# Scores, maxima and weighing of an attention stage in one tile shape of 64 rows by 32 columns, with two banks for the sums

## What is computed

```python
def _L0_xattn_ref(q, k, v, Wq, bq, Wk, bk, Wv, bv, Wo, bo):
    HEADS, D_K = 16, 16
    qh = (q @ Wq + bq).reshape(B, LQ, HEADS, D_K).transpose(0, 2, 1, 3)
    kh = (k @ Wk + bk).reshape(B, LKV, HEADS, D_K).transpose(0, 2, 1, 3)
    vh = (v @ Wv + bv).reshape(B, LKV, HEADS, D_K).transpose(0, 2, 1, 3)
    scores = jnp.einsum('bhqd,bhkd->bhqk', qh, kh) * scale
    attn = jax.nn.softmax(scores, axis=-1)
    ...
x = x + _L0_xattn_ref(_layernorm(x, axis=-1), ctx_512, ctx_512, ...)   # LQ = 256, LKV = 4096
```

## Time and profile before

| | us |
|---|---|
| median of three runs | 1431.7 |
| lowest and highest | 1428.06 and 1433.41 |
| profiled execution, its time | 1427.45 |
| profiled execution, its span | 1425.7 |
| PE busy | 1372.8 (96%) |
| DVE busy | 1070.9 (75%) |
| ACT busy | 962.1 (67%) |
| POOL busy | 287.7 (20%) |

### The profile page before, as it was taken

How to read it: one execution, slowest core, us unless ns; L and a number is a source line. 1 busy time by engine, 2 the same in 40 slices (tenths; PEclk the granted TensorE clock), 3 DMA queues, 4 the chain that set the end, 5 groups by cost and what they waited for, 6 DMA issues and landing times.

```text
span 1425.7 us, 32607 instructions
## 1 busy us (share of the span) xinstructions
PE 1372.8 (96%) x13186; PEld 757.5 (53%) x13186; DVE 1070.9 (75%) x2114; ACT 962.1 (67%) x1931; POOL 287.7 (20%) x321
## 2 busy tenths in 40 slices
PE   7799999999999999999999999998989999989998
PEld 4344444444444444444444545456547999856666
DVE  4787877778787778777778888835876768767757
ACT  5377777777777777777777666672896664448731
POOL 3353121222212222121222100000003100001210
PEclk9899999999999999999999999999999999999999
DMA  5865453335445335544424632002401320347000
GB/s 172 191 160 151 119 134 93 90 92 135 115 122 121 73 90 128 131 113 106 112 68 102 192 83 46 2 1 60 119 24 59 111 68 0 92 117 151 2 1 30
DMA packets 98790, 134.53 MB, mean 94 GB/s; under 512 B 11024, under 2 KB 74128, under 8 KB 92688
## 3 DMA queue, kind: packets, MB, share of 16 engines
q1 hardware_dynamic: 98640, 132.45, 36.8%
HBM read 94.15 MB, written 38.27 MB: 93 GB/s over the span
## 4 chain that ended last, share of the span: by engine, by line
PE 83%; DVE 7%; ACT 7%; issue 2%; DMA 1%; POOL 0%; SPq 0%; DVEq 0%; ACTq 0%; POOLq 0%
PE psum L546 19%; PE psum L566 18%; PE psum L527 7%; PE psum L592 4%; PE psum L632 4%; PE psum L2147 4%; PE psum L2121 3%; PE psum L1241 2%; PE psum L2866 2%; DVE peaks L693 1%; ACT probs L791 1%; ACT key_f L824 1%; PE psum L2876 1%; PE psum L275 1%; PE psum L1638 1%
## 5 line engine op out<-in xcount | busy, mean ns | idle before, releaser
L693 DVE TENSOR_REDUCE peaks<-psum 128x1 f32<-128x512 f32 x1024 | 654.6, 685 | 168.7 <-PE psum L527 157.1
L791 ACT ACTIVATE probs<-psum 128x512 f32<-128x512 f32 x1024 | 555.9, 595 | 126.8 <-PE psum L546 125.0
L546 PE MATMUL psum<-queriesT,keysT 64*128 64x256 bf16 (+1 forms) x4096 | 331.9, 272 | 11.0 <-ACT probs L791 9.8
L566 PE MATMUL psum<-probs,values 128*17 128x256 f32 x4096 | 320.5, 385 | 0.0
L546 PEld LDWEIGHTS psum<-queriesT,keysT 64*128 64x128 bf16 (+1 forms) x4096 | 171.9, 94 | 219.4 <-ACT probs L791 159.3
L527 PE MATMUL psum<-keysT,queriesT 64*128 64x512 bf16 x1024 | 210.2, 379 | 7.3 <-DVE peaks L693 4.0
L566 PEld LDWEIGHTS psum<-probs,values 128*17 128x17 f32 x4096 | 68.0, 95 | 160.4 <-issue 151.3
L927 POOL CAST key_parts<-key_f 128x512 bf16<-128x512 f32 x57 | 34.9, 612 | 516.0 <-ACT key_f L824 509.7
L592 PE MATMUL psum<-ctxT,wk 128*128 128x512 f32 x128 | 75.1, 670 | 2.2 <-DVE probs L736 0.9
L527 PEld LDWEIGHTS psum<-keysT,queriesT 64*128 64x128 bf16 x1024 | 59.8, 94 | 26.1 <-DVE peaks L693 17.5
L632 PE MATMUL psum<-wv,ctxT 128*128 128x256 f32 x256 | 72.0, 407 | 0.5 <-DVE probs L724 0.4
(11 more groups left out here) (315 smaller groups left out, 1647.7 us busy)
## 6 DMA issues: line engine op xcount, KB each, us to landing
keysT<-key_parts SPq DMA_DIRECT2D x186, 256.0 KB, 5.5
key_parts<-key_parts SPq DMA_DIRECT2D x90, 256.0 KB
ctx_nat<-in_ctx_dram SPq DMA_DIRECT2D x32, 256.0 KB, 3.2
ctx_in<-in_ctx_dram SPq DMA_DIRECT2D x24, 256.0 KB, 3.1
ctx_turned<-ctxT SPq DMA_DIRECT2D x24, 256.0 KB, 6.0
ctx_T<-ctx_turned SPq DMA_DIRECT2D x12, 512.0 KB, 3.9
qk_parts<-early_weights SPq DMA_DIRECT2D x24, 128.0 KB
q_parts<-q_parts SPq DMA_DIRECT2D x20, 128.0 KB
```

What stands on the lines that cost most here:

```text
L546: made = e.matmul(ps[j][:, e2 * S:(e2 + 1) * S], self.keysT[own, plane, i % RING, kt * P:(kt + 1) * P], self.queriesT[own, plane, u % 2, g ...
L566: made = e.matmul(k.bank(SUMS)[32 * quad:32 * quad + DH + 1, 0:S], self.values[b % 2][:, kt, g * GH + j, :], self.probs[:, (SLOTS * i + p) ...
L693: e.tensor_reduce(self.peaks[:, i % 2, j * QT + qt, c:c + 1], k.ps(("max", n)), AX.X, ALU.max).then_inc(*self.peaked.up(n))
L791: e.activation(self.probs[:, t % RINGP, 2 * j * S:(2 * j + 2) * S], k.ps(("scores", t, j)), ACT.Exp).then_inc(*self.exped.up((t, j)))
```

## The change

Scores, maxima and weighing all become matmuls of tiles with 64 rows and 32 columns. A score matmul of 128 keys is written as four of 32 (`STRIP`), a maximum of 128 queries as four of 32. Weighing of one slot is split over its 128 keys: first one half of the rows, then, behind a wait for it (`half_weighed`), the other, both adding to the same sums.

The order within a slot is new. One head is early and one late, in turn from slot to slot (`order`). PE writes the early head's first score step, the half of weighing on the other head's rows, the early head's three other steps, the maxima, two steps of the late head, the other half of weighing, and the last two steps. ACT takes the exponentials in the same order.

The sums have two banks, 3 and 4, in turn by group; copying them no longer holds up the next group's weighing. Three banks (5 to 7) are left for maxima and other jobs. DVE clears the second bank at slot 0. Both maxima of a pair now wait for their banks before either is written.

```diff
-SCORES, SUMS, BLOCK = (0, 1, 2), 3, 1
+HALVES, SUMS, STRIP = 3, (3, 4), P // 4
...
+def order(t):
+
+    return (0, 1) if t % 2 else (1, 0)
...
-            choice = (7, 0, 1, 2) if t < -1 else (4, 5, 6, 7)
+            choice = (7, 0, 1, 2) if t < -1 else (5, 6, 7)
...
-        def find_max(n, now):
-            i, j, qt, c = self.max_at(n)
+        def find_maxima(n, now):
+            ps = {}
+            for j in range(GH):
+                job, let_go = ("max", n + j), (self.peaked, n + j)
+                ps[j] = banks.use(4 + (n + j) % 3, w, job, let_go) if now < -1 else misc(now, job, let_go)
...
-            e.matmul(ps, self.queriesT[own, MAIN, u % 2, g, qt * P:(qt + 1) * P],
-                     self.keysT[own, MAIN, i % RING, c * BANK:(c + 1) * BANK],
-                     start=True, stop=True).then_inc(*self.max_made[j].up(n))
+            for col in range(0, P, STRIP):
+                for j in range(GH):
+                    own, q = slice(j * HALF, (j + 1) * HALF), qt * P + col
+                    made = e.matmul(ps[j][col:col + STRIP, :], self.queriesT[own, MAIN, u % 2, g, q:q + STRIP],
+                                    self.keysT[own, MAIN, i % RING, c * BANK:(c + 1) * BANK], start=True, stop=True)
+                    if col == P - STRIP:
+                        made.then_inc(*self.max_made[j].up(n + j))
+        def score(t, j, first, last):
+            i, p = divmod(t, SLOTS)
+            u, g = divmod(i, UNIT_GROUPS)
+            if first == 0:
+                banks.use((2 * t + order(t).index(j)) % HALVES, w, ("scores", t, j), (self.exped, (t, j)))
+            ps = k.ps(("scores", t, j))
+            for step in range(first, last):
+                e2, plane = divmod(step, 2)
+                kt, own = 2 * p + e2, slice(j * HALF, j * HALF + (TALL if plane == REST else HALF))
+                for col in range(0, P, STRIP):
+                    at = kt * P + col
+                    made = e.matmul(ps[col:col + STRIP, e2 * S:(e2 + 1) * S], self.keysT[own, plane, i % RING, at:at + STRIP],
+                                    self.queriesT[own, plane, u % 2, g, :], start=(plane == MAIN), stop=(plane == REST))
+            if last == 4:
+                made.then_inc(*self.scored[j].up((t, j)))
+        def weigh(v, half, begins, ends):
+            i, p = divmod(v, SLOTS)
+            b, g = divmod(i, NG)
+            own = slice(half * HALF, (half + 1) * HALF)
+            for e2 in range(2):
+                for j in range(GH):
+                    quad, at, kt = e2 * GH + j, 2 * j + e2, 2 * p + e2
+                    made = e.matmul(k.bank(SUMS[i % 2])[32 * quad:32 * quad + DH + 1, 0:S],
+                                    self.values[b % 2][own, kt, g * GH + j, :],
+                                    self.probs[own, v % RINGP, at * S:(at + 1) * S],
+                                    start=(p == 0 and begins), stop=(p == SLOTS - 1 and ends))
+            if begins:
+                made.then_inc(*self.half_weighed.up(v))
+            else:
+                made.then_inc(*self.weighed.up(v))
         for t in range(FIRST, TOTAL + 3):
             maxima = self.maxima(t)
-            if 0 <= t < TOTAL:
-                i, p = divmod(t, SLOTS)
-                u, g = divmod(i, UNIT_GROUPS)
-                w.wait_ge(self.shiftT_kept, i)
+            early, late = order(t)
+            due = self.weighings(t)
+            scoring = 0 <= t < TOTAL
+            if scoring:
+                w.wait_ge(self.shiftT_kept, t // SLOTS)
                 w.wait_ge(self.ones_in, 0)
-                ps = {}
-                for e2 in range(2):
-                    kt = 2 * p + e2
-                    for plane, rows in ((MAIN, HALF), (REST, TALL)):
-                        for j in range(GH):
-                            if j not in ps:
-                                ps[j] = banks.use(SCORES[(2 * t + j) % len(SCORES)], w, ("scores", t, j), (self.exped, (t, j)))
-                            own = slice(j * HALF, j * HALF + rows)
-                            made = e.matmul(ps[j][:, e2 * S:(e2 + 1) * S], self.keysT[own, plane, i % RING, kt * P:(kt + 1) * P],
-                                            self.queriesT[own, plane, u % 2, g, :], start=(plane == MAIN), stop=(plane == REST))
-                            if e2 and plane == REST:
-                                made.then_inc(*self.scored[j].up((t, j)))
-            for n in maxima:
-                find_max(n, t)
-            if (t - 1) % BLOCK == 0 and BLOCK + 1 <= t <= TOTAL + 1:
-                i, p0 = divmod(t - BLOCK - 1, SLOTS)
-                b, g = divmod(i, NG)
-                w.wait_ge(self.exped, (t - 2, 1))
-                for p in range(p0, p0 + BLOCK):
-                    w.wait_ge(self.v_kept, (b, p))
-                w.wait_ge(self.ones_set, b % 2)
-                if i:
-                    w.wait_ge(self.outT_kept, i - 1)
-                w.wait_ge(self.cleared, 0)
-                for p in range(p0, p0 + BLOCK):
-                    for e2 in range(2):
-                        for j in range(GH):
-                            quad, half, kt = e2 * GH + j, 2 * j + e2, 2 * p + e2
-                            made = e.matmul(k.bank(SUMS)[32 * quad:32 * quad + DH + 1, 0:S],
-                                            self.values[b % 2][:, kt, g * GH + j, :],
-                                            self.probs[:, (SLOTS * i + p) % RINGP, half * S:(half + 1) * S],
-                                            start=(p == 0), stop=(p == SLOTS - 1))
-                made.then_inc(*self.weighed.up((t - BLOCK - 1) // BLOCK))
+                score(t, early, 0, 1)
+            for v in due:
+                i, p = divmod(v, SLOTS)
+                w.wait_ge(self.exped, (v, order(v)[1]))
+                w.wait_ge(self.v_kept, (i // NG, p))
+                w.wait_ge(self.ones_set, i // NG % 2)
+                if i >= 2:
+                    w.wait_ge(self.outT_kept, i - 2)
+                w.wait_ge(self.cleared, 1)
+                weigh(v, 1 - early, True, False)
+            if scoring:
+                score(t, early, 1, 4)
+                if not due:
+                    score(t, late, 0, 4)
+            for n in maxima[::GH]:
+                find_maxima(n, t)
+            if scoring and due:
+                score(t, late, 0, 2)
+            for v in due:
+                w.wait_ge(self.half_weighed, due[-1])
+                weigh(v, 1 - late, False, True)
+            if scoring and due:
+                score(t, late, 2, 4)
...
-        banks.let_go[SUMS] = [(self.outT_kept, GROUPS - 1)]
+        for i in (GROUPS - 2, GROUPS - 1):
+            banks.let_go[SUMS[i % 2]] = [(self.outT_kept, i)]
         self.gather(e, w, banks.use(7, w, ("heads", GROUPS - 1), (self.heads_scaled, GROUPS - 1)), GROUPS - 1)
         return banks
+    def weighings(self, t):
+        return (t - 2,) if 2 <= t <= TOTAL + 1 else ()
...
+            if t == 0:
+                e.memset(k.bank(SUMS[1]), 0.0).then_inc(*self.cleared.up(1))
...
-                for j in range(GH):
+                for j in order(t):
                     w.wait_ge(self.scored[j], (t, j))
...
-                e.activation(self.outT[:, :], k.bank(SUMS)[:, 0:S], ACT.Copy).then_inc(*self.outT_kept.up(i))
+                e.activation(self.outT[:, :], k.bank(SUMS[i % 2])[:, 0:S], ACT.Copy).then_inc(*self.outT_kept.up(i))
```

More of the change, by code:

```diff
@@ L504, in tensor @@
         ident = k.ident
-        banks.let_go[SUMS] = [(self.cleared, 0)]
+        banks.let_go[SUMS[0]] = [(self.cleared, 0)]
         turn = 0
@@ L680, in vector @@
         e.tensor_copy(self.ident_b[:, :], k.ident).then_inc(*self.cleared.up("ident"))
-        e.memset(k.bank(SUMS), 0.0).then_inc(*self.cleared.up(0))
+        e.memset(k.bank(SUMS[0]), 0.0).then_inc(*self.cleared.up(0))
         self.norm_tiles(e, w, 0)
@@ L780, in scalar @@
                 if t >= RINGP:
[L781 removed]
+                    w.wait_ge(self.weighed, t - RINGP)
                 elif t == 0:
@@ L1083, in wait_first @@
         f = self.first
-        w.wait_ge(f.weighed, TOTAL // BLOCK - 1)
+        w.wait_ge(f.weighed, TOTAL - 1)
         w.wait_ge(f.outT_kept, GROUPS - 1)
```

13 lines of the change are left out of this document (5 added, 8 removed).

## The result

The changed kernel takes 1603.95 us (1602.52 to 1610.8), the kernel before 1430.06 on the same chip: 1.122 times as long, 95% interval 1.118 to 1.126. The forecast was 1363, faster. The profiled execution has a span of 1600.7 for 1425.7.

What follows compares the result with a forecast made beforehand. PE was taken to bound the changed loop. Savings of 33 (slots without another job), 18.5 (with one) and 15 us (group ends), 67 in all, took 1427.45 to 1360, as a median 1363; range 1340 to 1412.

Steps and rivals of the forecast that it cites:

- instructions: PE in each slot: 56 matmuls with loads for 26, needing 22 ns each; issuing them was put at no cost.
- the burst's rate: Weight loads on PE: eight start within 0.13 us, 5 ns each, taken as the rate for matmuls with loads.
- Rival C: Every slot: PE can't issue a matmul with load every 23.6 ns; at 27 ns the kernel takes 1520 us; chance 0.10.
- Slots without another job: Slots with no other job: DVE's two reduces set 1.22 us a slot, saving 33 us, bounds 15 to 38.
- The loop through the banks: Maxima banks, from matmul through reduce back to PE: 1.15 to 1.20 us, no tighter than DVE's 1.22.
- rival A: Slots without other jobs fall only to 1.28, others keep their time, group ends give 8: 1403 us; chance 0.14.
- Slots with another job: 185 slots where PE decides: one change of shape fewer, 0.10 us each, saving 18.5 us, bounds 9 to 28.
- Group ends: Slots after 26 group ends: the wait for the first exponential's bank goes, 0.58 us each, 15 us, bounds 5 and 16.
- The wait for the half: Weighing's second half waits for the first half's last matmul: taken as 0, maybe 0.1 us, 18 us at most.
- Second bank for sums: Weighing no longer waits for the copy of old sums; PE's matmuls waited 0.0 us there, so no gain.
- Independent halves: PE's row halves run independently, 1.067 us of array time each per slot; PE alone wants 1.10.
- Rival B: Matmuls start strictly in written order, 0.213 us more per slot, 1.31 a slot: 1427 us, no change; chance 0.05.

Runs made afterwards that it cites:

- the pads: Kernel before with 20 or 44 more one-column matmuls with loads per slot, directly ahead of weighing: 1498.77 and 1749.33 us.
- keys cut: Changed kernel, from the fourth group on reading 128 of 4,096 key columns, so later groups score old keys: 1498.15 us.
- 512-column scores: Changed kernel with 16 score matmuls of 512 columns per slot for 32 of 256, half of the keys unscored: 1499.76 us.
- three banks: Changed kernel with both keys cut and 512-column scores, its three banks for maxima and other jobs kept: 1422.99 us.
- four banks: Kernel of the three banks column, but with one bank for the sums and four for maxima and other jobs: 1401.17 us.
- a fourth score bank: Kernel before with four banks for scores and three for maxima and other jobs, no more instructions: 1420.95 us, ratio 0.993.

## Why the prediction was wrong

The step that failed is the one on *instructions*: "I take the burst's rate", 5 ns a pair where 22 are needed. The rate holds in a block (5.3 ns by the pads), but it answered the wrong question. What it lacked is a supply: 128 pairs in about 3.6 us are 28 ns a pair, above the 22 ns needed, and 56 pairs at 22 ns made PE stand still 86 times for 148.9 us. It also miscounted the pairs before, 18 and not 26. The page of before had the row that would have raised the question, 104 packets on q8 for 26,372 matmuls and loads, 254 to a packet; 56 pairs in 1.22 us would use such a packet up in 2.8 us. Rival C had the right side and even nearly the threshold (23.6 ns a pair), but that is luck: its mechanism, a fixed issue time for each pair, isn't there, since strips start 3 to 7 ns apart.

The sum of the loop, from the first score of slot 0 to that of slot 511, by the earlier trace rows's kinds of slots, in us, with the last two kernels of the changed order (keys cut, 512-column scores). For the slots with values and with other jobs together (452.7 before) the forecast was 419, its 18.5 and its 15 at group ends taken off:

| | before | forecast | after | of it stops | three banks | four banks |
|---|---|---|---|---|---|---|
| 326 without another job | 442.6 | 409.6 | 500.3 | 78.5 | 414.5 | 413.6 |
| 48 with values | 128.5 | | 117.9 | 0.4 | 116.2 | 117.0 |
| 137 with other jobs | 324.2 | | 445.8 | 69.6 | 356.3 | 330.8 |
| loop | 895.3 | 829 | 1063.9 | 148.4 | 887.0 | 861.3 |

- **Stops.** Put at nothing, they are 148.4 of the 168.6 us that the loop grew. Without them the loop of after is still 915 where that with three banks is 879 less its own stops. I take these 37 us to be lost behind stops, with ACT and DVE dry and PE's clock lower (0.81 granted from 238 to 247, in the stop shown), but no run shows it by itself, nor how much is the clock's.
- **Slots without another job.** 33 us forecast, 28 found once the stops are gone. The size was right, the mechanism half: not 1.22 throughout, but 1.11 behind a slot in which DVE had time, and 1.29 to 1.32 in a row. "The loop through the banks is no tighter", 1.15 to 1.20, failed: it is 1.31, mostly because a bank given back takes 0.15 to PE's next start (I had 0.05) and 0.47 from there to the reduce (0.42). That is rival A's mechanism, and its 1.28, the median with three banks.
- **Slots with another job.** 18.5 us forecast, with bounds of 9 to 28; what came was a loss, 37 us with three banks and stops nearly gone (472.5 less the 435 that 452.7 is without the gain at group ends). With values they take 2.34 or 2.47 for 2.42, with keys 2.47 for 2.38. They did lose one of three changes of shape, but maxima and the job itself wait for one of three banks. With four banks slots with values take 2.34 to 2.37, near the forecast's 2.32, but those with keys 2.37, 0.01 under before, and the other common kinds gain 0.01 to 0.05: the 0.10 a slot came in no kernel. Some 14 slots stay slower by 0.2 to 1.5 even with four; seven of them are third slots of a group, where the copy of the sums holds them up, and the others I haven't traced.
- **Group ends.** 15 us forecast; slots that begin a group fell by 17 (82.0 to 64.7), 3.00 to 2.34 for single ones. Right, and had more cheaply by a fourth score bank.
- **The wait for the half.** 0 forecast, 18 at most. It is 0.15 in many slots (381 waits, 62.3 us with four banks, 107 and 20.8 with three), seen where DVE doesn't decide.
- **Second bank for sums, third bank fewer for maxima.** Both put at nothing: "PE's matmuls wait 0.0 us ahead of L566". Nearly true of the old order, in which the copy hides behind maxima (the loads of L566 wait 9.0 us for it, in the same rows); in the new one it costs about 30 us with one bank, and giving it a second one at the maxima's expense costs 22 net (1401 to 1423). 861.3 less 30 is 831 for the loop, where the forecast had 829. That agreement is luck: slots without another job would be 391 where it had 410, the others 440 where it had 419. And no kernel has both banks: three for scores, two for sums and four for maxima would be nine.
- **Independent halves.** Right. Scores and weighing start 0.04 apart on their own rows, and a slot of 1.118 here (1.108 with 512-column scores) is the 1.067 of columns with 0.04 to 0.05 to spare. Rival B, and the rule of the Trainium skill (TensorE: Matmul & The Clock Gate, "Packing small matmuls — row/col tiling") that it goes by, don't fit: by that rule no slot would be under 1.31. (The prediction's working of it for the old weighing was too high: starts in the order written still allow neighbouring column tiles side by side, about 5 x 0.213 = 1.07 us and not 1.7; against 0.56 the conclusion stands.)

```profile
240.29 0.41 PE L566 MATMUL psum<-probs,values 64*17 64x256 f32 x4
240.33 0.40 PE L553 MATMUL psum<-queriesT,keysT 64*32 64x256 bf16 x8
```

On what was missing, the Trainium skill (Runtime: NRT & Kernel Launch, "Instruction fetch mechanics") does say that instructions are refilled in blocks of 16 KiB, 256 instructions, and the packets here agree. It also says that crossing a block is mostly hidden because engines dispatch more slowly than the blocks arrive; here 86 crossings cost 148.9 us.

## What to carry to other kernels

Before splitting matmuls into smaller tiles, divide: instructions of PE (matmuls and loads both) per us of the target, against one block of 256 in about 3.6 us with quiet DMA queues, and 5 to 8 with large reads in flight (blocks that ended in a stop of over 2 us lasted 5.3 to 8.3). 40 pairs in 1.3 us were bearable with short key reads (8.3 us of stops) and not with full ones (68.3), and 18 were never felt. A wait called "issue" that lasts over 1 us and returns every 256 instructions was this. And a bank that an order doesn't need by its waits of today may be the one that the next order needs: count each bank's loop (its release, the matmul, the reader) in the order that is planned.

## What the runs showed of the hardware

- PE's instructions came in packets of 16,384 bytes, 256 instructions. Where PE had stopped, the next packet started 1.13 us or more after it resumed (nine times in ten), and PE resumed about 1.4 us (1.26 to 1.60) after a landing. Blocks that ended in a stop lasted 3.2 us at the shortest, 4.6 in the median.
- Data transfers delay these packets: the same kernel stood still for 148.9 us with full key reads and for 82.6 with short ones.
- Row and column tiles took their matmuls independently: two halves of rows with four strips each ran 1.067 us of columns in 1.108 to 1.118, strips starting 3 to 7 ns apart.
- A change of tile shape on PE cost about 0.12 us: one more per slot took it from 1.325 to 1.446, all but 0.01 of it between the last score step and the maxima.
- A bank went back from DVE to PE in 0.15 us (end of the reduce to the start of the next matmul into it), and from that start to the next reduce it was 0.47.
